# A gated delta-rule layer with a mixture of experts: the last level of the block inverse on 64x64 tiles of TensorE

## The reference, cut to what matters

```python
def step(S, inputs):
    q_t, k_t, v_t, g_t, b_t = inputs
    S = S * jnp.exp(g_t)[..., None]
    kv = jnp.einsum('bhd,bhdv->bhv', k_t, S)
    delta = b_t[..., None] * (v_t - kv)
    S = S + k_t[..., None] * delta[:, :, None, :]
    o = jnp.einsum('bhd,bhdv->bhv', q_t, S)
    return (S, o)
```

## Time and profile before

| | us |
|---|---|
| median of 3 runs | 6376.87 (6365.69 to 6393.16) |
| the profiled execution's own time | 6372.03 |
| its span in the profile | 6370.3 |

### The profile page before, as it was taken

How to read it: one execution, slowest core, us unless ns; L and a number is a source line. 1 busy time by engine, 2 the same in 40 slices (tenths; PEclk the granted TensorE clock), 3 DMA queues, 4 the chain that set the end, 5 groups by cost and what they waited for, 6 DMA issues and landing times.

```text
span 6370.3 us, 128595 instructions
## 1 busy us (share of the span) xinstructions
PE 5917.3 (93%) x38912; PEld 4849.9 (76%) x38912; DVE 4167.3 (65%) x10433; ACT 3223.1 (51%) x6704; POOL 2018.3 (32%) x2752
## 2 busy tenths in 40 slices
PE   7999999999999999999999999999999999899999
PEld 5887777878787777777787878787777778755555
DVE  5766666666666666666676666667666666555555
ACT  4555555555555555555555555555555555411111
POOL 3333333333333333333333333333333333200000
PEclk9999999999999999999999999999999999999999
DMA  2000000000000000000000000000000000000000
GB/s 74 18 17 14 18 18 14 17 18 17 15 18 18 17 14 18 17 15 18 17 17 15 18 14 18 18 17 17 15 18 17 14 18 16 26 11 10 10 10 14
DMA packets 55174, 112.22 MB, mean 18 GB/s; under 512 B 5088, under 2 KB 38112, under 8 KB 54496
## 3 DMA queue, kind: packets, MB, share of 16 engines
q1 hardware_dynamic: 54624, 105.42, 5.3%
HBM read 97.01 MB, written 8.39 MB: 17 GB/s over the span
## 4 chain that ended last, share of the span: by engine, by line
issue 37%; PE 35%; POOL 18%; ACT 7%; DVE 2%; POOLq 1%; DVEq 0%; ACTq 0%
POOL kl L314 8%; PE bank L1133 8%; PE bank L1088 6%; PE bank L938 5%; PE bank L1105 3%; PE bank L1143 3%; POOL T L329 3%; POOL e_sb L340 3%; POOL e_sb L343 3%; ACT L512 2%; POOL TT L333 2%; PE bank L956 2%; PE bank L983 2%; ACT vs L442 2%; PE bank L968 1%
## 5 line engine op out<-in xcount | busy, mean ns | idle before, releaser
L314 POOL TENSOR_TENSOR kl<-kl,tot 128x256 f32<-128x256 f32 x768 | 503.6, 656 | 1787.0 <-PE bank L938 1773.4
L938 PE MATMUL bank<-kq,kl 128*128 128x128 f32 x6144 | 858.7, 283 | 75.6 <-DVE AT L637 53.0
L938 PEld LDWEIGHTS bank<-kq,kl 128*128 128x128 f32 x6144 | 752.6, 192 | 122.0 <-issue 74.6
L978 PEld LDWEIGHTS bank<-lx,TT 128*128 128x128 f32 x5120 | 630.6, 191 | 195.3 <-ACT lx L416 134.6
L956 PE MATMUL bank<-T,lx 128*128 128x64 f32 x6144 | 772.3, 268 | 0.0
L921 PE MATMUL bank<-xT,par 128*128 128x512 f32 x1536 | 766.8, 595 | 0.8 <-ACT gaT L397 0.8
L956 PEld LDWEIGHTS bank<-T,lx 128*128 128x128 f32 x6144 | 748.2, 192 | 0.0
L978 PE MATMUL bank<-lx,TT 128*128 128x64 f32 x5120 | 681.0, 276 | 55.4 <-ACT lx L416 35.9
L968 PE MATMUL bank<-ident,T 128*128 128x128 f32 x3072 | 482.5, 280 | 159.7 <-DVE T L659 159.7
L429 ACT ACTIVATE TT<-bank 128x256 f32<-128x256 f32 x768 | 295.8, 385 | 551.4 <-PE bank L968 550.0
L434 ACT ACTIVATE W<-bank 128x128 f32<-128x128 f32 x512 | 142.1, 278 | 784.4 <-PE bank L1019 784.4
(11 more groups left out here) (165 smaller groups left out, 12826.4 us busy)
## 6 DMA issues: line engine op xcount, KB each, us to landing
par<-params_dram SPq DMA_DIRECT2D x128, 519.0 KB, 3.5
wo<-wo_dram SPq DMA_DIRECT2D x128, 128.0 KB, 2.0
xall<-x_dram SPq DMA_DIRECT2D x16, 512.0 KB, 3.9
out_dram<-xall SPq DMA_DIRECT2D x16, 512.0 KB, 2.9
lx<-ffn_dram SPq DMA_DIRECT2D x1, 3456.0 KB, 11.7
wfa_sb<-wfa_dram SPq DMA_DIRECT2D x1, 128.0 KB, 2.2
wga_sb<-wga_dram SPq DMA_DIRECT2D x1, 128.0 KB, 2.0
wb_sb<-wb_dram SPq DMA_DIRECT2D x1, 8.0 KB, 2.0
```

The lines of the kernel that those rows point to most:

```text
L314: pool.tensor_tensor(halves(kl[:, :], h)[:, :, 0, :], src, totr.broadcast_to([P, SEQ // (2 * h), h]), ALU.mult).then_inc(s["kl_ready"], 1)
L938: ins = pe.matmul(dst[:, :, n], chunk(left, n), right[:, :, n, :, 1, :], start=True, stop=True)
L978: ins = pe.matmul(b_x[:, 256 + n * HALF:256 + (n + 1) * HALF], chunk(TT[pB], n), XS[:, n * HALF:(n + 1) * HALF], start=True, stop=True)
```

## The change

At the last level, both products are written on a 64x64 tile of the array. `lt_times_t(6)` takes rows 0 to 63 and columns 64 to 127 of LT[6] as stationary operand, rows 0 to 63 of T's first 64 columns as moving operand, and writes partitions 64 to 127 of b_x; its place in the array is row 0, column 64. ScalarE copies only these 64 partitions to XW. The second product takes rows 64 to 127 of XW and of TT and writes partitions 0 to 63 of b_y, at row 64, column 0 of the array. VectorE subtracts only those 64 partitions from TT. The number of matmuls and their place in PE's order stay as they are; each moves 64 columns as before. The stationary operands have 64 rows and 64 columns in place of 128 and 128. Ahead of each of the two groups PE's sequencer adds 1 to a new semaphore, `pe_go`, for which nobody waits. All other products remain on the whole array.

```diff
+def upper(t):
+
+    return t[:, :].rearrange("p (n two h) -> p n two h", n=NCH, two=2)[0:HALF, :, 1, :]
...
                     act.wait_ge(s["zero_ok"], 1)
                     after(act, s["yw_mm"], iB)
-                    h = 1 << l
-                    act.activation(halves(XW, h)[:, :, 0, :], b_x[:, 0:SEQ // 2].rearrange("p (m h) -> p m h", h=h),
-                                   ACT.Copy).then_inc(s["x_ev"], 1)
+                    act.activation(XW[HALF:P, :].rearrange("p (n two h) -> p n two h", n=NCH, two=2)[:, :, 0, :],
+                                   b_x[HALF:P, 0:SEQ // 2].rearrange("p (n h) -> p n h", n=NCH), ACT.Copy
+                                   ).then_inc(s["x_ev"], 1)
...
-                    tr = halves(TT[pB][:, :], h)[:, :, 1, :]
+                    tr = upper(TT[pB])
                     dve.wait_ge(s["yw_mm"], iB + 1)
                     dve.wait_ge(s["tt_ev"], (LEVELS - 1) * (iB + 1))
-                    dve.tensor_tensor(tr, tr, b_y[:, 0:256].rearrange("p (m h) -> p m h", h=h),
+                    dve.tensor_tensor(tr, tr, b_y[0:HALF, 0:256].rearrange("p (n h) -> p n h", n=NCH),
                                       ALU.subtract).then_inc(s["tt_upd"], 1)
...
+                    if l == LEVELS - 1:
+                        pe.sem_inc(s["pe_go"], 1)
                     for n in range(NCH):
-                        ins = pe.matmul(b_x[:, n * HALF:(n + 1) * HALF].rearrange("p (m h) -> p m h", h=h),
-                                        chunk(LT[l], n), halves(chunk(T, n), h)[:, :, 0, :], start=True, stop=True)
+                        if l == LEVELS - 1:
+                            ins = pe.matmul(b_x[HALF:P, n * HALF:(n + 1) * HALF],
+                                            LT[l][0:HALF, n * P + HALF:(n + 1) * P], T[0:HALF, n * P:n * P + HALF],
+                                            start=True, stop=True, tile_position=(0, HALF))
+                        else:
...
+                    pe.sem_inc(s["pe_go"], 1)
                     for n in range(NCH):
-                        ins = pe.matmul(b_y[:, n * HALF:(n + 1) * HALF].rearrange("p (m h) -> p m h", h=h),
-                                        chunk(XW, n), halves(chunk(TT[pB], n), h)[:, :, 1, :], start=True, stop=True)
+                        ins = pe.matmul(b_y[0:HALF, n * HALF:(n + 1) * HALF], XW[HALF:P, n * P:n * P + HALF],
+                                        TT[pB][HALF:P, n * P + HALF:(n + 1) * P], start=True, stop=True,
+                                        tile_position=(HALF, 0))
                     ins.then_inc(s["yw_mm"], 1)
```

More of the change, by code:

```diff
@@ L138, in delta_moe @@
         ogT = sb("ogT", [P, SEQ])
-        names = """pool_go dve_go sp_go x_in w_in consts halves_ok ident_ok zero_ok wo_in0 wo_in1 par_in0 par_in1 amp_ok
+        names = """pe_go pool_go dve_go sp_go x_in w_in consts halves_ok ident_ok zero_ok wo_in0 wo_in1 par_in0 par_in1 amp_ok
         bn_st bn_mv bn_var bn_rs xn_ok xnT_mm xt_ev fa_mm ga_mm be_mm fa_ev ga_ev be_ev be_one beta_ok
@@ L954, in lt_times_t @@
                         pe.wait_ge(s["x_ev"], (LEVELS - 1) * iB + l - 1)
+                    if l == LEVELS - 1:
+                        pe.sem_inc(s["pe_go"], 1)
                     for n in range(NCH):
-                        ins = pe.matmul(b_x[:, n * HALF:(n + 1) * HALF].rearrange("p (m h) -> p m h", h=h),
-                                        chunk(LT[l], n), halves(chunk(T, n), h)[:, :, 0, :], start=True, stop=True)
+                        if l == LEVELS - 1:
[3 more added lines that the diff above has]
+                        else:
+                            ins = pe.matmul(b_x[:, n * HALF:(n + 1) * HALF].rearrange("p (m h) -> p m h", h=h),
+                                            chunk(LT[l], n), halves(chunk(T, n), h)[:, :, 0, :],
+                                            start=True, stop=True)
                     ins.then_inc(s["x_mm"], 1)
```

## The result

The changed kernel takes 6419.18 us, the median of 5 runs (6417.86 to 6423.23), against 6380.39 (6365.69 to 6393.16) for the kernel before: a ratio of 1.0062, 95% interval 1.0044 to 1.0079. I had forecast 6358, in a range of 6320 to 6408. It is slower by 0.6%, not faster, and outside the range.

A forecast was written before the change was run, and what follows sets the result against it. PE, busy 93% of 6370.3 us, was taken as the bound. Gains of 15 us (second group) and 2 (first) gave 6355 from the profiled 6372, or 6360 from the runs' median; forecast 6358, 8-in-10 range 6320 to 6408.

The forecast's parts named there:

- Which groups count: Last level: second product's gain counts whole, 128 times; first product's is waited away in 98 of 128 supersteps, counting in 30.
- The loads: Weight loads of both groups: half the columns load in half the time, 0.056 us a pair; gain 0.34 us a group.
- The switches: Whole array to tile and back: 0.11 us each, half a full drain, leaving a group gain of 0.12 us.
- A full drain: Rival at each group's two switches: array empties, costing 0.44 us; group loses 0.10 us, total 6387; chance 0.18.
- VectorE's cover: Behind the second product: VectorE can follow a gain up to about 0.6 us per superstep; its L611 wait (0.31) should shrink.
- `pe_go` at nothing, VectorE and ScalarE at their old times: Semaphore increment ahead of each group costs nothing; ScalarE's copy and VectorE's subtraction keep their time on half the partitions.
- The clock: TensorE throughout: clock stays at 2.4 GHz in practice, no stretch idle long enough to alter that; no cost counted.
- my rivals: For both groups: free switch 6323, chance 0.25; full drain 6387, 0.18; no effect 6372 to 6377, 0.07; drain, long pairs 6473, 0.15.
- the 0.18 on slower: Whole kernel: chance of at least half a percent (32 us) slower, from drain with long pairs (0.15) and full drain's tail.
- The sum: Whole kernel: second group 15 us plus first group 2 us gained, 6372 - 17 = 6355 against the profiled execution.
- theory 2: Follow-up experiments' theory, not the forecast's: the shorter superstep period brings TensorE's clock down (rhythm), rather than less array activity.

## Why the prediction was wrong, point by point

- **Which groups count.** Right. The second product's saving is in the period (41.25 with the second alone or both), the first adds nothing to it (41.34 with the first alone). But I had the first group gain 0.12 us and the idle time before the sums grow by it. It gained 0.01 (1.33 in place of 1.34), and the idle time stayed at 0.38: there was nothing to be waited away.
- **The loads.** Right. A tile's load is 134 ns in place of 192, and the 58 ns less are the half of the 0.1125 us per pair read from the earlier trace rows.
- **The switches.** Nearly right, and the guess in it was lucky. I had a gain of 0.34 us without switches and took 0.11 for each switch. The superstep got 0.085 us shorter, so two switches cost 0.34 - 0.085 = 0.255, against 0.22 assumed, 0 and 0.44 as bounds. No run shows the 0.34 by itself. The starts of the single matmuls say nearly the same: the first of the tile 0.09 late, the second another 0.05, the first transpose behind 0.04 and the second 0.055 more, 0.24 together. The Trainium skill ("TensorEngine Tiling (Array Packing)", Key Properties) says that changing the mode drains the engine. The trace agrees that going in and out costs time; whether the array drains in full it doesn't show. A full drain as I had built it from the records' tails would be 0.44.
- **VectorE's cover.** Held as to the time: what the group saves is in the period. But I had expected VectorE's wait at level 0, 0.31 us, to shrink, and it didn't. In VectorE's timeline of the changed kernel (L616 is the old L611) both waits are what they were:

```profile
2215.99 0.67 DVE L788 TENSOR_TENSOR xall<-xall,bank 128x512 f32 x1
2216.83 0.69 DVE L788 TENSOR_TENSOR xall<-xall,bank 128x512 f32 x1 [0.17 <-PE bank L1120]
2217.83 0.86 DVE L616 SCALAR_TENSOR_TENSOR lx<-bank,sc,mask 128x64 f32<-128x64 f32 x4 [0.31 <-PE bank L943]
```

  The first addition starts 2.08 us behind the second product's start (2215.99 - 2213.91), where it was 2.25 before (2195.92 - 2193.67), and level 0's eviction 3.92 in place of 4.10. The whole row of VectorE's work has moved forward with PE. What it gave up lies ahead of the first addition: its waits for the second product's result are 4.1 us in all, where they were 13.4.
- **`pe_go` at nothing, VectorE and ScalarE at their old times.** No run contradicts it; the increment alone wasn't tried.
- **The clock. Here it failed.** "The clock is at its upper level, 2.4 GHz, in practice throughout, and I see no stretch that becomes idle long enough to alter that." The first half rested on a row in tenths: 9 stands for anything from 0.9, and the mean was 0.991, 57 us of lost speed, 0.9% of the time and larger than any gain I discussed. The second half looked only for idle time, and the idle times did stay at 0.60 and 0.38. What changed was the work between them: 8 pairs of 0.11 us became 8 of 0.058. I had named the first product's place myself, between two waits, and drew from it only that its gain was waited away. The same fact made it harmful: between two waits, less work brought the clock down and could gain nothing. The first product alone on tiles cost 56 us. The mechanism wasn't among my rivals, so the 0.18 on slower stood on wrong ones.
- **The sum.** -17 us was forecast against the profiled execution. Measured: -11 from the shorter supersteps, about +60 from the clock, a term that I had put at nothing, +51 in the span.

The Trainium skill ("TensorE: Matmul & The Clock Gate", Part 1) has the clock follow how busy TensorE has lately been. That rule bears on this change and I left it out, having found no longer idle time. The runs agree with it: filling the two waits takes the mean clock from 0.981 to 0.992.

## What to carry to other kernels

Where TensorE waits behind a group, making that group shorter can't gain time, and it can lose some: here a product beside the path cost 56 us of 6371 by the clock alone. Read the mean granted clock to three digits, and ask of each shortened PE group what PE does in the few us around it. If the clock is the price, work that nobody uses, put into the waits, can be worth more than the work saved (6419 to 6350 us); moving real work there would be better still, which wasn't tried.

## What the runs showed of the hardware that I had not expected

- Going from the whole array to a 64x64 tile and back costs some 0.24 to 0.255 us together, worked out as above. The eight pairs of the tile group, with the way out, take 0.61 us (2213.91 to 2214.52).
- A stretch of lower clock that falls on the sums costs 1.63 us, and there were 23 more stretches for the first product alone, which is 0.84 us of 41.
- Small differences in the work between two waits go with many more falls. At nearly equal matmul time (2.42 and 2.35 us in the stretch ahead of the sums) and equal waits, 2.04 against 1.67 us of weight loading went with 0 and with 11 falls in 78 regular supersteps. Which part of the work counts isn't shown: loading, streaming and the share of the array changed together. Nor is it shown why 67 supersteps with the same work and waits kept the clock; the place of a superstep in the clock's own rhythm, as in theory 2, may still choose among them.
